# Splitting the six score banks of a softmax attention two and four instead of three and three

## What is computed

```python
mixed = x @ Wqkv.T                       # q, k, v of 16 heads
attn = jnp.einsum('gqd,gkd->gqk', q, k) * norm
attn = jax.nn.softmax(attn, axis=-1)     # exp(s - max(s)) / sum
ctx = jnp.einsum('gqk,gkd->gqd', attn, v)
out = ctx @ Wproj.T + bproj
```

## Time and profile before

| | us |
|---|---|
| median of three runs | 1172.69 (1171.26 to 1176.45) |
| the profiled execution, its own time | 1177.77 |
| its span, first to last instruction | 1176.0 |
| the steps of the softmax stage, first L441 to its last one | 41.7 to 264.1 |
| mean granted clock of TensorE | 0.983 of full speed |

### The profile page before, as it was taken

One profiled execution on the slowest core, in us unless ns is written; L12 is line 12 of the kernel. 1 busy time (PEld: TensorE's weight loads), 2 busy tenths in 40 slices (PEclk: granted clock), 3 DMA queues, 4 the chain that ended last, 5 costly groups with the idle time before them and its releaser, 6 DMA issues. The chain is left out here.

```text
span 1176.0 us, 22452 instructions
## 1 busy us (share of the span) xinstructions
PE 1127.3 (96%) x7559; PEld 907.9 (77%) x7559; DVE 932.3 (79%) x2126; ACT 773.7 (66%) x1535; POOL 635.6 (54%) x1077
## 2 busy tenths in 40 slices
PE   8999999987998899999999999999999999999788
PEld 7444434336666799999999999999999999999776
DVE  6988887836558888888888888888888888888762
ACT  3477677762447676767676777777777777676533
POOL 4020500000705777786777686777687777767630
PEclk9999999987999999999999999999999999999899
DMA  6333333300320112102111211211211211010020
GB/s 184 55 55 56 55 55 56 55 2 2 115 70 20 35 48 68 48 33 77 40 48 33 84 33 48 68 48 34 80 37 39 78 33 47 33 48 33 32 72 1
DMA packets 23449, 60.50 MB, mean 51 GB/s; under 512 B 3367, under 2 KB 8359, under 8 KB 22183
## 3 DMA queue, kind: packets, MB, share of 16 engines
q1 hardware_dynamic: 23335, 59.07, 18.8%
HBM read 44.67 MB, written 2.33 MB: 40 GB/s over the span
## 5 line engine op out<-in xcount | busy, mean ns | idle before, releaser
L1804 DVE SCALAR_TENSOR_TENSOR ln_xn<-l_proj_q,par,ln_xn 128x511 f32<-128x511 f32 (+2 forms) x192 | 142.6, 743 | 98.0 <-ACT ln_xn L1688 95.6
L698 DVE TENSOR_REDUCE a_neg_max<-a_scores 128x1 f32<-128x512 f32 x244 | 154.9, 683 | 31.2 <-PE a_scores L419 29.4
L617 ACT ACTIVATE a_probs<-a_scores_t 128x512 f32<-128x512 f32 x256 | 138.3, 600 | 59.5 <-PE a_scores_t L441 58.4
L1694 ACT ACTIVATE ln_xn<-ln_xn,par 128x512 f32<-128x512 f32 x128 | 92.6, 723 | 93.3 <-DVE ln_xn L1804 93.3
L1388 POOL TENSOR_TENSOR l_k_tok<-l_normed,k_norm 128x384 f32<-128x384 f32 x64 | 65.0, 1016 | 153.8 <-ACT l_normed L1705 151.9
L1804 DVE SCALAR_TENSOR_TENSOR ln_xn<-l_proj_k,par,ln_xn 128x511 f32<-128x511 f32 (+2 forms) x192 | 143.2, 746 | 4.5
L1705 ACT ACTIVATE l_normed<-l_turn_q,l_shift,l_scale 128x128 f32<-128x128 f32 x252 | 94.8, 457 | 22.3 <-POOL l_shift L1381 22.3
L1379 POOL TENSOR_TENSOR l_scale<-l_small,l_minus_half 128x8 f32<-128x8 f32 x64 | 105.0, 1641 | 5.0
L1705 ACT ACTIVATE l_normed<-l_turn_k,l_shift,l_scale 128x128 f32<-128x128 f32 x252 | 95.6, 480 | 0.0
L1762 ACT ACTIVATE l_gate<-l_proj_gv 128x512 f32<-128x512 f32 x64 | 38.2, 597 | 79.1 <-PE l_proj_gv L1476 79.1
L1578 PE MATMUL l_outp<-l_masked,l_values 128*128 128x128 f32 x512 | 88.6, 275 | 1.0 <-issue 1.0
(11 more groups left out here) (369 smaller groups left out, 3622.7 us busy)
## 6 DMA issues: line engine op xcount, KB each, us to landing
l_keep<-keep_rows SPq DMA_DIRECT2D x64, 448.0 KB, 3.5
a_stack<-a_dense SPq DMA_DIRECT2D x90, 128.0 KB, 4.3
head_raw<-w_heads SPq DMA_DIRECT2D x8, 1024.0 KB, 6.7
x_tok<-x SPq DMA_DIRECT2D x4, 512.0 KB, 8.3
wo_raw<-w_o SPq DMA_DIRECT2D x1, 2048.0 KB, 11.4
out<-x_tok SPq DMA_DIRECT2D x1, 1920.0 KB
a_stack<-a_max_rows_t SPq DMA_DIRECT2D x64, 4.0 KB
ctx_tok<-w_qkv SPq DMA_DIRECT2D x1, 768.0 KB, 6.8
```

The costliest lines, as they stand in the source:

```text
L617: act.activation(probs[:, n % 2, h, :], scores_t[(4 * n + h) % TURNS][:], ACT.Exp, scale=SOFT_SCALE).then_inc(probs_done, 1)
L698: dve.tensor_reduce(neg_max[:, g % 2, at:at + 1], max_bank(g, j), AX.X, ALU.max, negate=True).then_inc(max_done, 1)
L1694: act.activation(conv[:, w, m, :], conv[:, w, m, :], ACT.Silu, bias=par[:, h, 2 * TAPS + w:2 * TAPS + w + 1]).then_inc(act_sem[w], 1)
L1804: ins = dve.scalar_tensor_tensor(conv[:, w, m, s:], proj[w][:, 0:SEQ - s], par[:, h, tap:tap + 1], conv[:, w, m, s:], ALU.mult, ALU.add)
```

## The change

The six banks are split two and four: `scores`, for the maxima, becomes a ring of `MAX_TURNS = 2`, and `scores_t`, for the transposed tiles, a ring of `TURNS = 4`. So tile n of the maxima now waits for the reduction of tile n - 2, and transposed tile q for the exponential of tile q - 4. The first 24 tiles of maxima still use all six banks in turn. `stack_banks` and `xt` name other banks of the six. No instruction is added or removed, and each engine has its instructions in the same order as before; only the banks' names and what is waited for differ.

```diff
-    TURNS = 3
+    MAX_TURNS, TURNS = 2, 4
@@ softmax_attention
         scores_t = [psum(f"a_scores_t{i}", [P, SEQ]) for i in range(TURNS)]
-        scores = [psum(f"a_scores{i}", [P, SEQ]) for i in range(TURNS)]
+        scores = [psum(f"a_scores{i}", [P, SEQ]) for i in range(MAX_TURNS)]
@@
-        stack_banks = scores_t[0], scores[2], scores_t[1], scores_t[2]
+        stack_banks = scores_t[1], scores_t[0], scores_t[2], scores_t[3]
@@ max_bank
-            return first_scores[n % len(first_scores)][:] if n < wide_tiles else scores[n % TURNS][:]
+            return first_scores[n % len(first_scores)][:] if n < wide_tiles else scores[n % MAX_TURNS][:]
@@ last_use
-            return n - TURNS if n >= wide_tiles + TURNS else last_wide(n % TURNS)
+            return n - MAX_TURNS if n >= wide_tiles + MAX_TURNS else last_wide(n % MAX_TURNS)
@@
-        xt = [[scores_t[1 + k][:] for k in range(KD)]]
+        xt = [[scores_t[2 + k][:] for k in range(KD)]]
@@ probs_chunk
                     if q < TURNS:
-                        pe.wait_ge(max_done, last_wide(TURNS + q) + 1)
+                        pe.wait_ge(max_done, last_wide(MAX_TURNS + q) + 1)
                     else:
                         pe.wait_ge(probs_done, q - TURNS + 1)
```

## The result

The changed kernel takes 1199.92 us (median of four executions, 1197.41 to 1202.85) against 1174.57 us for the kernel before: **1.0229 times as long, 95% interval 1.0207 to 1.0251**, 25.4 us slower. In a second batch, of five executions, it was 1199.40 against 1173.39 us, 1.0218 (1.0204 to 1.0232), 26.0 us slower. Two executions among all that follow, one of the kernel before (clock 0.748) and one of `warm_filled_33` (clock 0.848), took over 6% longer than the others of their kernel, and the ratios leave them out.

What follows compares the result with a forecast made beforehand. PE was taken as the bound, 96% busy. Seam terms 13.7 + 4.1 + 4.3 = 22.1 us, less 0.3 in the last six steps, gave +21.8 on the median 1172.7: 1194.5 us, range 1187 to 1201 (chance 0.80).

Steps and rivals of the forecast that it cites:

- (a): Seams of two steps without other work on PE, 23 steps: context 0.59 us later in the row, sum 13.7 us.
- (b): Seams with four transposes, steps 1 and 5, 13 steps: context 0.60 us later in the row, sum 4.1 us.
- (c): Seams with a projection, 22 steps: steps 2 covered by another wait, some others late, sum 4.3 us.
- The sum over the stage: Lateness at all three kinds of seam in the softmax stage, added up: 22.1 us of growth.
- The last six steps: the fourth bank gives 0.3 us: Stage's end, steps without maxima, bounded by ACT: the fourth transposed bank saves 0.3 us.
- Nothing before 44 us and nothing behind the stage changes but its start: Everything outside the softmax stage: no change in length, only a later start behind it.
- a sign of being wrong: Outside the stage: a difference of more than 3 us would count against the prediction.
- The clock as a rival: PE's new idle spots at seams lower the granted clock; one group slowed costs 10.4 us, 1205 us; chance 0.08.
- At most 12.0 us from the fourth bank: Seams where the second transposed tile waits for an exponential: 20 waits of 0.60 us, the most to be had.
- the rival's price: Rival that the transposed ring was the bind at the seam: 12.0 us less, 1160.7 us; chance 0.02.
- The rule on weight loads: PE's loads pulled ahead at some 44 late steps would save 4 us, 1190 us; rejected from the trace.
- The base of the sum: Profiled execution's 1177.8 us stood 5.1 us above the median 1172.7; the forecast was taken against the median.

Runs made afterwards that it cites:

- warm_filled_33: Kernel before (three and three banks) with other work moved to the seams and throw-away matmuls in the last six steps; 1167.02 us, 0.9953.
- filled_24: Changed kernel with three blocks of other work of steps 3, 5 and 7 moved to bare seams; 1187.64 us, 1.0121 of the kernel before.
- before_again: The kernel before, unchanged, run once more for a second trace; 1173.19 us, 1.0002.
- before_late: Kernel before with 95 more throw-away matmuls ahead of the first transposed tile, so everything behind stands later; 1195.47 us, 1.0206.
- warm_24: Changed kernel with throw-away matmuls in idle places of the last six steps; 1196.82 us, 1.0207 of the kernel before.
- after_short: Changed kernel with each maximum taken over only the first 64 of 512 keys; 1169.62 us, 0.9951 of the kernel before.
- filled_33: Kernel before with three blocks of other work of steps 3, 5 and 7 moved to bare seams; 1168.43 us, 0.9952.
- three_two: Against the kernel before, three maxima banks kept and only two transposed banks used in turn; 1193.26 us, 1.0151.

## Why the prediction was right and wrong

**The seam (a), right.** Forecast for a bare seam: tiles together, the maxima's second at 1.55, the context at 1.97. Measured 0.00, 1.54, 1.97. Steps without other work in group 7 were late by 1.1 and 0.35 as forecast: step 2 grew from 2.32 to 3.46 us, step 3 from 3.20 to 3.54.

**Seams with other work (b) and (c), right.** The context of group 4's step 1 stands at 1.29 behind its seam, forecast 139.76 - 138.47 = 1.29. Steps 2, forecast as covered by the wait for DVE's subtraction, last 3.78 to 3.79 us as before. The row that answers to the earlier trace rows, group 4's step 2 of the changed kernel, shows how the lateness eats the idle time, from 0.49 to 0.17:

```profile
156.55 0.50 PE L375 MATMUL a_misc<-xn_hi,a_w_hi 128*128 128x512 f32 x1 [0.17 <-DVE a_dense L680]
```

**The sum over the stage, right.** 22.1 us forecast, 22.24 measured; group 4 +3.08 (3.0), group 5 +2.42 (2.4), group 7 +4.12 (4.2).

**"The last six steps: the fourth bank gives 0.3 us", wrong, small.** They take 21.65 us with either split at full clock (`filled_24`, `before_again`). ACT bounds them, as the sentence itself said.

**"Nothing before 44 us and nothing behind the stage changes but its start", the step that failed.** This term of the sum was put at nothing without a reason; it measured 3.1 and 3.8 us (25.4 and 26.0 less the stage's 22.2), beyond the 3 us that the prediction itself had named as a sign of being wrong. What the runs show in its place is a lower granted clock.

The executions of the kernel before, 52 in three batches and in `before_again`, had a mean clock of 0.982 to 0.994, in the middle 0.991; the nine of the changed kernel 0.980 to 0.988, in the middle 0.985. Among these nine the time goes from 1197.4 us at 0.987 to 1202.85 at 0.980, some 0.7 us for each 0.001. By this estimate the 0.006 between the kernels is about 4 us, the size of what is missing: 22.2 + 4 = 26. Executions at the same mean clock bear it out: at 0.985 the kernel before took 1177.11 us once and the changed one 1198.81 to 1199.61; at 0.990 four of the former took 1171.92 to 1173.62 and one of the latter 1196.87. Such pairs are 22 to 25 us apart, less than the medians.

Traces show where the clock is low (the last six steps and behind them), but those of the two batches are of their shortest executions, and they account for some 1.5 of the 3 to 4 us. Why the clock falls there more often stays open. That everything stands 22 us later is the better supported candidate: `before_late` took some 2 us more than its delay, and its trace has the falls at the same places, but its interval also allows none of it. That PE is emptier in the stage and in the last steps is another, for which `warm_24` shows no gain beyond its interval.

**The clock as a rival, right in kind, wrong in size and place.** I gave it 0.08 and 10.4 us for a whole group at half clock. It came as 1.2 and 3.6 us inside the stage in two of six traces, and as a few us behind it. The Trainium skill, "TensorE: Matmul & The Clock Gate", section "A second HAM failure mode: psum-queue depth-cycling", says that idle spots from cycling through PSUM banks can make the clock swing. The stretch at 170 us, at clock 0.51 after one in which PE was busy for 3.34 of 4.00 us, is such a fall, in one of the three single traces; no run shows that the cycling through banks is what brought it.

**"At most 12.0 us from the fourth bank", and the rival's price, wrong.** With the reductions made short, `after_short` got 1.1 us of it. I priced a wait by its length without asking what is late next. The context waits for the exponential right behind the one that the tile waits for, and the row at 134.59 shows it: at most 0.27 us a seam, 20 x 0.27 = 5.4 us by this estimate, not 12.0. The chance of 0.02 for that rival was fair; its 1160.7 us was not to be had even with a free reduction.

**The rule on weight loads.** The prediction held that a load doesn't run ahead of a wait for a reduction. The row at 146.02 agrees: the load starts 0.05 us after the reduction's end, and the context follows the lone tile after 0.43 us, not 0.33.

**The base of the sum.** The execution that I read ran most of its last six steps at half clock, which cost 4.65 us there. Taking the forecast from the median put that right in the number. But the row also showed that the stretch behind the stage differs by several us between executions of one kernel, and I priced that only as a rival inside the stage, and put what is behind it at nothing.

## What to carry to other kernels

A ring of two between engines where both tiles of a pair are consumed by one slower engine ties the producer to the consumer's *second* result; a wait that looks long on the other ring says nothing about where a bank is best spent. Ask of each bank which wait ends last with it and without it, at each kind of step: here the answers, added up over 58 steps, came within 0.14 us of the measured growth of the stage. And before pricing a wait that goes away, find the next thing that is released by the same chain; the cheap gain was not a bank but to move three blocks of other work into the gap (`filled_33`, 0.9952).

## What the runs showed of the hardware

The mean granted clock differed by some thousandths between kernels of nearly the same instructions, and between executions of one kernel: 0.982 to 0.994 for the kernel before, in the middle 0.991, and 0.980 to 0.990 for the changed one, in the middle 0.985. In `three_two` one execution at 0.992 took 1185.2 us and three at 0.979 to 0.981 took 1193.1 to 1194.1, 8 us more. A difference of half a per cent between two such kernels need not come from their instructions; the stretches at full clock, compared one by one, tell.
